# Queries and keys of a four-layer conditioned sequence kernel: from tile to tile instead of through HBM scratch, with a new order of the work

## The chip, the cores and the metric

The kernel runs on 1 core of one Trainium2 chip. The metric is the device time of one execution in microseconds (us), lower is better. Engines are named TensorE (PE), VectorE (DVE), ScalarE (ACT), GpSimd (POOL) and SyncE (SP, which only issues DMAs here).

## The reference

The input x has 16 batches of 256 rows and 256 columns, with a conditioning vector of 64 and one of 256 per batch. Four layers follow each other; nothing passes between batches.

```python
# L0: weights of the batch from a hypernetwork
Wd_b = Wd + 0.1 * (h_lang @ Wdd.T + bdd);  Wu_b = Wu + 0.1 * (h_lang @ Wdu.T + bdu)
x = x + relu(x @ Wd_b.T + bd) @ Wu_b.T + bu
# L1: LayerNorm with weight and bias, plus tanh(cond @ lin_w.T + lin_b), weight and bias again
# L2: 16 heads of 16 columns, all weights shared, gates g1 b1 g2 b2 a1 a2 from the conditioning
h = layernorm(x) * g1 + b1;  q, k, v = split(h @ W_qkv.T + b_qkv)
x = x + (softmax(q @ k.T / 4) @ v @ W_o.T + b_o) * a1
h = layernorm(x) * g2 + b2
x = x + (gelu_tanh(h @ W_f1.T + b_f1) @ W_f2.T + b_f2) * a2          # 1024 wide
# L3: RMSNorm with a scale of the batch, gated GELU, activations rounded to 8 bits, ternary weights
val, gate = split(h @ up_w.T);  y = quant(val * gelu(gate)) @ ternary(down_w).T + x
```

## The kernel before

**Stages and turns.** A batch passes four stages: A (L0, L1 and the queries, keys and values), B (attention), C (output projection and feed-forward of L2) and D (L3). Turn t works on batch t in A, t-1 in B, t-2 in C and t-3 in D, so there are 19 turns: turns 3 to 15 have all four stages, turns 0 to 2 fill the pipeline and turns 16 to 18 drain it. Steps have names such as `A.q` (the queries' product) or `C.f0` (first quarter of the feed-forward's first product). In what order each engine takes the steps is written out by hand in the strings `HEAD` (turns 0 to 5), `FULL` (one turn, repeated from 6 to 12) and `TAIL` (the rest); each engine waits on semaphores and works in its order.

**Precision.** Most products are done on fp32r pairs: a high part (ACT copies it) and a low part (DVE or POOL subtracts), three products for one (`three`, L528). The weights of L2 and L3 are split in this way in turns 0 to 2: `W.qkv`, `W.fa` (first feed-forward weight), `W.up` (128x4096), `W.f2` (POOL, one instruction), and the ternary weight (`W.abs`, `W.tern`).

**Queries and keys.** The scores are one product over 4 x 16 = 64 rows of `Qp` against `Kp`: row 4i is the high part of head row i, 4i+1 and 4i+2 pair high and low parts, and row 4i+3 of `Qp` first holds zero and later the maximum of the score row (`B.m`, which comes back through `mt`), against ones in `Kp`. `B.s` makes the scores for the maximum (eight pairs of heads, in four steps, L658; DVE reduces each pair, L1180), `B.t` makes them again, with the maximum subtracted, for the exponential (L680, ACT L902), `B.o` weights the values (L692). To interleave the rows, SP stores the parts to `qk_scratch` in HBM (`A.qs`, `A.ks`: four DMAs) and loads them back (`A.ql0` to `A.kl3`: eight DMAs of 256 KB, 128 partitions each). PE's `B.s0` waits for the two DMAs of heads 0 (`heads_in[0]`).

**The start.** The batch's L0 weights are generated ahead of turn 0: 16 chunks of 1 MB (`hyper`) are loaded, multiplied (`generate`, L538), copied to `gen`, and the rows of batch 0 and 1 go from `gen` to `cur` and `second` (`first_rows`, L381 and L382, 8 partitions each). `store_rows` (L422) writes `gen` to HBM for the other batches. `A.down` (L596) waits for `cur_ready`; `A.up` is L602, `A.ht` (transposes) L609. `C.proj`, the first step of C, is L703, and marks a turn below.

Of the kernel before, what the change touches and what calls it, by code (L numbers as in the profile page):

```python
# [5 lines left out]
F32 = mybir.dt.float32  # L6
F32R = mybir.dt.float32r
BF16 = mybir.dt.bfloat16
ALU = mybir.AluOpType
# [3 lines left out]
P = 128  # L13
NB = 16
# [50 lines left out]
def at(steps, name, b):  # L65
# [8 lines left out]
        0: W.store0 A.load W.f0 W.up A.qs A.ks A.ql0 A.kl0 A.ql1 A.kl1 A.kl2 A.ql2 A.ql3 A.kl3 1: W.late B.m0 2: C.tc 1: A.load B.m1 A.qs A.ks A.ql0  # L74
        A.kl0 A.kl1 A.kl2 A.ql1 A.kl3 A.ql2 A.ql3 2: B.m0 A.load A.qs B.m1 A.ks A.ql0 A.kl0 3: C.tc 2: A.kl1 A.ql1 A.kl2 A.ql2 A.ql3 A.kl3 3: A.load
        B.m0 A.ks B.m1 A.qs A.kl0 D.y0 A.ql0 4: C.tc 3: A.ql1 A.ql2 D.y1 A.ql3 A.kl1 A.kl2 A.kl3 4: B.m0 A.load A.qs B.m1 A.ks A.ql0 A.kl0 A.kl1
        A.ql1 5: C.tc 4: D.y0 A.kl2 D.y1 A.ql2 A.kl3 A.ql3 5: B.m0 A.load A.qs B.m1 A.ks D.y0 A.ql0 A.kl0 6: C.tc 5: A.ql1 A.ql2""",
    "PE": """
        0: A.down A.up A.ht A.q A.k A.v 1: A.down A.up B.s0 B.s1 A.ht B.m0 B.s2 B.s3 A.q A.k B.m1 B.t0 B.t1 B.o0 B.t2 B.t3 B.o1 A.v 2: C.proj A.down
        A.up B.s0 C.ht B.s1 C.f0 C.f1 C.f2 C.f3 B.m0 A.ht B.s2 W.abs B.s3 A.q A.k B.m1 B.t0 A.v C.g0 B.t1 C.g1 B.o0 C.g2 B.t2 C.g3 B.t3 3: A.down 2:  # L80
        B.o1 C.xt 3: B.s0 A.up C.proj D.u0 B.s1 D.u1 C.ht D.u2 C.f0 C.f1 C.f2 C.f3 B.m0 A.ht B.s2 D.u3 B.s3 D.qt0 A.q A.k B.m1 D.y0 B.t0 A.v C.g0
        B.t1 C.g1 D.qt1 B.o0 C.g2 B.t2 C.g3 B.t3 D.y1 B.o1 C.xt 4: A.down B.s0 C.proj D.u0 A.up D.u1 C.ht B.s1 D.u2 C.f0 C.f1 C.f2 C.f3 B.m0 A.ht
        B.s2 D.u3 B.s3 A.q D.qt0 A.k D.y0 B.m1 A.v B.t0 C.g0 B.t1 C.g1 D.qt1 B.o0 C.g2 B.t2 C.g3 B.t3 D.y1 B.o1 C.xt 5: A.down B.s0 C.proj D.u0 A.up
        D.u1 C.ht B.s1 D.u2 C.f0 C.f1 C.f2 C.f3 B.m0 A.ht B.s2 D.u3 B.s3 D.qt0 A.q A.k""",
    "ACT": """
        0: W.qkv A.down A.lnb A.ht A.q W.fa A.k A.v 1: A.down W.up A.lnb A.ht A.q B.t0 B.t1 B.t2 B.t3 A.k W.f2 B.t4 B.t5 B.t6 B.t7 A.v 2: A.down
        C.lnb C.ht C.f0 C.f1 A.lnb C.gh0 C.f2 A.ht C.f3 A.q C.gh1 A.k B.t0 B.t1 B.t2 B.t3 A.v B.t4 B.t5 B.t6 B.t7 3: A.down 2: C.xt 3: D.u0 C.lnb
        D.u1 C.ht D.u2 C.f0 C.f1 A.lnb C.gh0 C.f2 A.ht D.u3 C.f3 D.qt0 A.q C.gh1 A.k B.t0 B.t1 B.t2 B.t3 D.qt1 A.v B.t4 B.t5 B.t6 B.t7 C.xt 4: D.u0
        A.down C.lnb D.u1 C.ht D.u2 C.f0 C.f1 A.lnb C.gh0 C.f2 A.ht D.u3 C.f3 A.q D.qt0 A.k C.gh1 B.t0 B.t1 A.v B.t2 B.t3 D.qt1 B.t4 B.t5 B.t6 B.t7
        C.xt 5: A.down D.u0 C.lnb D.u1 C.ht D.u2 C.f0 C.f1 A.lnb C.gh0 C.f2 A.ht D.u3 C.f3 D.qt0 A.q C.gh1 A.k B.t0 B.t1 B.t2 B.t3 A.v D.qt1 B.t4  # L90
        B.t5 B.t6 B.t7 C.xt 6: A.down D.u0 C.lnb D.u1 C.ht D.u2 C.f0""",
    "DVE": """
        0: A.up A.lna A.lng A.ln A.cur W.qkv A.q A.k 1: W.fa A.up A.lna A.lng A.ln W.up B.s0 B.s1 B.s2 B.s3 B.p0 B.m0 B.s4 B.s5 B.s6 B.s7 B.p1 B.m1
        A.cur A.q B.o1 A.k B.o3 2: C.proj C.ln A.up B.s0 A.lna A.lng B.s1 B.s2 B.s3 A.ln W.abs B.p0 B.m0 B.s4 B.s5 B.s6 B.s7 B.p1 B.m1 A.q A.k
# [74 lines left out]


def cond_seq_kernel(nc, xT, x, hyper, base, cols, k64, rows, w_qkv, w_o, w_f1, w_f2, w_up, w_down, out,
                    rows_scratch, cur_scratch, qk_scratch):
    ctx = ExitStack()
    with ctx:
        def sb(name, shape, dt):
# [1337 lines left out]
```

## Time and profile before

| | |
|---|---|
| median of 3 runs | 881.86 us (879.83 to 883.41) |
| profiled execution | 881.95 us, span 880.1 us |
| PE busy | 798.5 us, 91% of the span |
| DVE, ACT, POOL busy | 555.9, 554.7, 324.1 us |
| mean granted TensorE clock | 0.943 of full speed |
| DMA | 118.50 MB in 56207 packets |

The span is the time from the first to the last instruction of one profiled execution; its own time is 1.85 us longer. All times in rows are us from the span's start. The granted clock has two levels, 0.5 and 1.00 of full speed (1.2 and 2.4 GHz). SP's DMA issues are not counted as busy time, but its queue (SPq) has rows of its own: start and duration of each issue.

### The profile page before, as it was taken

What the parts mean: (1) busy time and instruction counts of PE and PEld (TensorE: products, weight loads), DVE (VectorE), ACT (ScalarE), POOL (GpSimd) and SP (SyncE); (2) the same over time, 40 slices, a digit from 0 to 9 for tenths busy, and PEclk for the clock granted to TensorE, in tenths of its full rate; (3) what the DMA queues carried; (4) which work ended last, traced back from release to release, by engine and by line L of the source; (5) the groups of instructions that cost most, each with busy time, mean ns of one, the idle gap of its engine ahead of it and who ended that gap; (6) DMA issues with size and microseconds to landing.
All of it is one profiled execution on the core that took longest, in us unless ns stands there. A gap on an engine that the chain in (4) does not pass through costs nothing.

```text
span 880.1 us, 16405 instructions
## 1 busy us (share of the span) xinstructions
PE 798.5 (91%) x6108; PEld 634.1 (72%) x6108; DVE 555.9 (63%) x1063; ACT 554.7 (63%) x844; POOL 324.1 (37%) x398
## 2 busy tenths in 40 slices
PE   6753377999999999999999999999999999999977
PEld 4103256778787878787878788888788887877664
DVE  1313856677767768585858585858586867675424
ACT  1012343668695858685867777676868676867652
POOL 1003423253534344443434352625252535232330
PEclk9855767999999999999999999999999999999998
DMA  9989633434243332425151515141524423220000
GB/s 344 386 325 355 260 127 109 145 106 136 97 136 112 128 121 99 150 86 163 69 179 50 195 49 170 56 171 59 168 77 153 143 96 106 106 94 9 25 13 12
DMA packets 56207, 118.50 MB, mean 135 GB/s; under 512 B 6112, under 2 KB 11616, under 8 KB 53424
## 3 DMA queue, kind: packets, MB, share of 16 engines
q1 hardware_dynamic: 56128, 117.46, 38.6%
q8 instruction: 48, 0.79, 0.4%
q14 instruction: 31, 0.25, 0.1%
HBM read 82.23 MB, written 34.16 MB: 132 GB/s over the span
## 4 chain that ended last, share of the span: by engine, by line
PE 77%; DVE 5%; issue 5%; ACT 4%; POOL 4%; DMA 4%; SPq 1%; POOLq 0%; DVEq 0%; ACTq 0%
PE bank L528 41%; PE pair_s L692 6%; PE pair_t L528 5%; PE bank L789 3%; PE pair_s L680 3%; PE bank L703 3%; DMA hyp<-in_hyper 2%; PE pair_s L658 2%; PE bank L781 2%; PE pair_t L680 2%; PE bank L596 2%; PE bank L602 1%; DVE nmax L1180 1%; PE pair_t L658 1%; DVE hd L1248 1%
## 5 line engine op out<-in xcount | busy, mean ns | idle before, releaser
L1398 POOL TENSOR_TENSOR G_lo<-G,G_hi 128x512 fp32r<-128x512 f32 x64 | 81.9, 1293 | 117.6 <-ACT G_hi L922 117.6
L528 PE MATMUL bank<-wup_hi,hD_hi 128*128 128x512 f32 x256 | 110.5, 432 | 3.8 <-POOL hD_lo L1371 3.1
L528 PE MATMUL bank<-wup_lo,hD_hi 128*128 128x512 f32 x256 | 101.8, 397 | 0.0
L528 PE MATMUL bank<-wup_hi,hD_lo 128*128 128x512 f32 x256 | 101.7, 397 | 0.0
L902 ACT ACTIVATE Pr<-pair_s 128x1024 f32<-128x1024 f32 x64 | 65.7, 1027 | 44.3 <-PE pair_s L680 44.0
L1408 POOL TENSOR_TENSOR x<-x,gated 128x512 f32<-128x512 f32 x16 | 20.4, 1274 | 165.6 <-DVE gated L1238 165.6
L1180 DVE TENSOR_REDUCE nmax<-pair_s 128x4 f32<-128x1024 f32 x64 | 77.9, 1217 | 4.5 <-PE pair_s L658 4.2
L1180 DVE TENSOR_REDUCE nmax<-pair_t 128x4 f32<-128x1024 f32 x64 | 77.7, 1214 | 0.0
L528 PE MATMUL bank<-wf_hi,G_hi 128*128 128x256 f32 x256 | 76.9, 300 | 0.9 <-ACT G L917 0.8
L1204 DVE STREAM_TRANSPOSE oq<-pair_s 128x512 f32<-128x512 f32 x32 | 22.9, 717 | 78.8 <-PE pair_s L692 78.8
L949 ACT ACTIVATE gl<-bank,rsD 128x512 f32<-128x512 f32 x64 | 43.7, 683 | 45.2 <-PE bank L528 44.9
L528 PE MATMUL bank<-wf_lo,G_hi 128*128 128x256 f32 x256 | 71.7, 280 | 0.0
L528 PE MATMUL bank<-wf_hi,G_lo 128*128 128x256 f32 x256 | 71.7, 280 | 0.0
L1248 DVE SCALAR_TENSOR_TENSOR hd<-bank,rsD,gl 128x512 f32<-128x512 f32 x64 | 47.8, 746 | 33.7 <-PE bank L528 25.6
L692 PE MATMUL pair_s<-Pr,Va 128*32 128x256 f32 x1024 | 64.9, 396 | 1.0 <-ACT Pr L902 0.9
L902 ACT ACTIVATE Pr<-pair_t 128x1024 f32<-128x1024 f32 x64 | 65.3, 1021 | 0.0
L528 PEld LDWEIGHTS bank<-wup_hi,hD_hi 128*128 128x128 f32 x256 | 48.5, 189 | 18.2 <-POOL hD_lo L1371 3.4
L528 PEld LDWEIGHTS bank<-wup_lo,hD_hi 128*128 128x128 f32 x256 | 48.5, 190 | 11.8
L528 PEld LDWEIGHTS bank<-wup_hi,hD_lo 128*128 128x128 f32 x256 | 48.8, 191 | 9.7
L528 PEld LDWEIGHTS bank<-wf_hi,G_hi 128*128 128x128 f32 x256 | 48.2, 188 | 8.1 <-issue 2.5
L957 ACT ACTIVATE qT<-bank 128x1024 bf16<-128x1024 bf16 x32 | 32.7, 1023 | 26.0 <-PE bank L781 26.0
L692 PEld LDWEIGHTS pair_s<-Pr,Va 128*32 128x32 f32 x1024 | 29.8, 113 | 26.1 <-ACT Pr L902 7.9
(192 smaller groups left out, 2251.7 us busy)
## 6 DMA issues: line engine op xcount, KB each, us to landing
hyp<-in_hyper SPq DMA_DIRECT2D x16, 1024.0 KB, 10.0
Qp<-qk_scratch SPq DMA_DIRECT2D x64, 256.0 KB, 4.7
Kp<-qk_scratch SPq DMA_DIRECT2D x64, 256.0 KB, 4.6
qk_scratch<-q_hi SPq DMA_DIRECT2D x16, 512.0 KB, 2.8
qk_scratch<-k_hi SPq DMA_DIRECT2D x16, 512.0 KB, 3.2
tC<-rows_scratch SPq DMA_DIRECT2D x16, 384.0 KB, 4.5
xT_t<-in_xT SPq DMA_DIRECT2D x16, 256.0 KB, 4.5
x_t<-in_x SPq DMA_DIRECT2D x16, 256.0 KB, 4.6
```

The costliest lines, as they stand in the source:

```text
L528: mm = pe.matmul(dst, l, r, start=first and i == 0, stop=last and i == 2)
L658: mm = pe.matmul(pair[p % 2][:, half, r * L:(r + 1) * L], Qp[lo:lo + KR, 1 - par, p, r * P:(r + 1) * P], Kp[lo:lo + KR, 1 - par, p, :], st ...
L680: mm = pe.matmul(pair[p % 2][:, half, k * L:(k + 1) * L], Kp[lo:lo + KR, 1 - par, p, k * P:(k + 1) * P], Qp[lo:lo + KR, 1 - par, p, :], st ...
L692: mm = pe.matmul(bank[1][32 * j:32 * j + 32, (g % 2) * L:(g % 2 + 1) * L], Va[:, 1 - par, k, VW * (4 * g + j):VW * (4 * g + j) + 2 * DH], ...
L703: mm = pe.matmul(bank[5][:, r * D:(r + 1) * D], oT[:, k, r * P:(r + 1) * P], wo[:, k, :], start=k == 0, stop=k == KT - 1)
L789: mm = pe.matmul(bank[6][:, 0:D], qT[:, k, :], wq3[:, k, :], start=k == 0, stop=k == FT - 1)
L902: act.activation(Pr[:, p % 4, :, :].rearrange("p a n -> p (a n)"), pair[p % 2][:, :, :].rearrange("p a n -> p (a n)"), ACT.Exp, scale=DH * ...
L949: act.activation(gl[:, n % 2, :], bank[6][:, :], ACT.Gelu, scale=rsD[:, 1, n // 2:n // 2 + 1]).then_inc(act_d, 1)
L957: act.activation(qT[:, :, :].rearrange("p k n -> p (k n)"), bank[7][:, :].bitcast(BF16), ACT.Copy).then_inc(act_d, 1)
L1180: dve.tensor_reduce(nmax[:, n % 2, :, p % GP, :], pair[p % 2][:, :, :].rearrange("p a (r n) -> p a r n", r=RT), AX.X, ALU.max, negate=True ...
L1248: dve.scalar_tensor_tensor(hd[:, (n % 2) * HALF:(n % 2 + 1) * HALF], bank[7][:, :], rsD[:, 1, n // 2:n // 2 + 1], gl[:, n % 2, :], ALU.mul ...
L1398: pool.tensor_tensor(G_lo[:, 2 * i:2 * i + 2, :], G[:, 2 * i:2 * i + 2, :], G_hi[:, 2 * i:2 * i + 2, :].bitcast(F32), ALU.subtract).then_i ...
```

## The change

1. Queries and keys: `qk_scratch` goes. SP copies each part straight from `q_hi`, `q_lo`, `k_hi`, `k_lo` into the interleaved rows of `Qp` and `Kp`, 32 partitions to every fourth partition, 64 KB each: 8 DMAs for `A.qh0`, 4 for `A.ql0`, 8 for `A.kh0`, 4 for `A.kl0`, and 2 small ones that zero the maximum's rows again, so 26 in place of 12. ACT and DVE now guard `q_hi` and the others by PE's last `B.s` of the batch before.
2. Rows: the 16 issues for `second` leave the loop ahead of turn 0 and come in turn 0 (`W.second0`); the load of `wqkv_raw` goes behind the last `first_rows`.
3. Weight splits: `W.up`, the first feed-forward weight, `W.f2` on POOL and the ternary rounding are cut in 2 to 4 pieces each and put at other places; `W.up`'s load comes behind `A.kl0` of turn 0. `W.qkv` on DVE waits for POOL's `nb1`.
4. Unused products: `keep_busy(n)` issues n float32 products of 128x256 on TensorE, whose result nobody reads, in the generation loop and in turn 0.
5. New `HEAD`, `FULL` and `TAIL` for all engines.

```diff
 FULL "SP":
-        -1: A.kl1 D.y1 A.kl2 A.ql3 A.kl3 0: B.m0 A.load A.qs B.m1 A.ks D.y0 A.ql0 A.kl0 1: C.tc 0: A.ql1 A.ql2""",
+        -1: A.qh0 B.m1 A.kh0 A.kl0 D.y0 0: C.tc -1: A.ql0 D.y1 0: B.m0 A.load""",
 FULL "PE" (turned round; one step moved):
-        ... C.g1 B.o0 D.qt1 C.g2 B.t2 ...
+        ... C.g1 D.qt1 B.o0 C.g2 B.t2 ...
 FULL "DVE" (turned round; one step moved):
-        ... D.quant1 D.y0 B.o1 A.cur C.g3 D.y1 B.o3 ...
+        ... D.quant1 B.o1 D.y0 A.cur C.g3 D.y1 B.o3 ...
 HEAD "SP":
-        0: W.store0 A.load W.f0 W.up A.qs A.ks A.ql0 A.kl0 A.ql1 A.kl1 A.kl2 A.ql2 A.ql3 A.kl3 1: W.late B.m0 2: C.tc 1: A.load B.m1 ...
+        0: W.f0 W.zero0 W.store0 W.second0 A.load A.qh0 A.ql0 A.kh0 A.kl0 W.up 1: A.load B.m0 W.late A.qh0 B.m1 A.ql0 2: C.tc 1: A.kh0 A.kl0 2: ...
 HEAD "DVE":
-        ... 1: W.fa A.up A.lna A.lng A.ln W.up B.s0 B.s1 B.s2 B.s3 B.p0 B.m0 B.s4 B.s5 B.s6 B.s7 B.p1 B.m1 A.cur A.q B.o1 A.k B.o3 2: C.proj C.ln A.up B.s0 ...
+        ... 1: A.up A.lna A.lng A.ln B.s0 B.s1 B.s2 B.s3 B.p0 B.m0 B.s4 B.s5 B.s6 B.s7 B.p1
+        B.m1 W.fone1 A.cur W.upper0 A.q W.upper1 B.o1 A.k W.upper2 B.o3 W.upper3 2: C.proj B.s0 C.ln A.up A.lna B.s1 ...
 HEAD "PE":
-        2: C.proj A.down A.up B.s0 C.ht B.s1 C.f0 C.f1 C.f2 C.f3 B.m0 A.ht B.s2 W.abs B.s3 A.q A.k ...
+        2: C.proj B.s0 A.down A.up C.ht B.s1 C.f0 C.f1 C.f2 B.m0 W.abs A.ht B.s2 C.f3 B.s3 A.q A.k ...
 TAIL "PE", turns 15 and 16: A.v of turn 15 now between C.xt and the next C.proj
...
+            def zero_rows():
+                sp.wait_ge(zero, 6)
+                sp.dma_start(none_scratch, x3[0:2, 0].rearrange("p r n -> p (r n)").unsqueeze(1).to_broadcast([2, 4, HALF])).then_inc(planes_out, 16)
+                for u in range(2):
+                    for j in range(4):
+                        sp.dma_start(Qp[3:P:4, u, 2 * j:2 * j + 2, :].bitcast(F32), x3[0:32, 0]).then_inc(planes_out, 16)
...
+            def place(dst, part, rows, par):
+                for j in range(4):
+                    for r in rows:
+                        sp.dma_start(dst[r:P:4, par, 2 * j:2 * j + 2, :].bitcast(F32), part[32 * j:32 * j + 32, :, :].bitcast(F32)).then_inc(heads_in[j], 16)
...
+                    elif (stage, what) == ("A", "qh"):
+                        past(sp, pe_t, PE_T, f"t{NP - 1}", a, 2)
...
+                        for half in range(2):
+                            sp.dma_start(Qp[64 * half + 3:64 * half + 8:4, par, :, :].rearrange("p c n -> p (c n)").bitcast(F32),
+                                         none_scratch.rearrange("q j n -> q (j n)")).then_inc(heads_in[0], 16)
                         sp.wait_ge(act_a, at(ACT_A, "qhi1", a))
+                        place(Qp, q_hi, (0, 1), par)
...
+            def keep_busy(n):
+                for _ in range(n):
+                    pe.matmul(bank[7][:, 0:D], ident, wo[:, 0, :], start=True, stop=True)
             for c in range(6, NCH):
                 generate(c)
+                keep_busy(1 if c < NCH - 1 else 6)
...
                     mm.then_inc(pe_a, 1)          # a_up: keep_busy(15) if a == 0; a_ht: keep_busy(4) if a == 0
...
-                    pe.wait_ge(heads_in[n], 32 * b + 32)
+                    pe.wait_ge(heads_in[n], (128 if n == 0 else 96) * (b + 1))
```

## Rows read from the trace of the kernel before

**Rows 1.** The page: busy time and share, granted clock in 40 slices.
```profile
PE 798.5 (91%) x6108; PEld 634.1 (72%) x6108; DVE 555.9 (63%) x1063; ACT 554.7 (63%) x844; POOL 324.1 (37%) x398
...
PEclk9855767999999999999999999999999999999998
```
**Rows 2.** Windows: length, busy PE PEld DVE ACT POOL, clock, DMA share, GB/s.
```profile
44.00:66.00 22.00, 11.61 (x48) 2.18 (x44) 3.37 (x5) 3.27 (x4) 1.32 (x1) 0.50 0.90 325
...
88.00:110.00 22.00, 8.76 (x49) 5.95 (x48) 18.12 (x25) 8.64 (x11) 8.84 (x8) 0.71 0.70 260
...
132.00:154.00 22.00, 16.69 (x102) 13.81 (x91) 14.82 (x29) 7.42 (x14) 8.26 (x14) 0.78 0.33 109
...
220.00:242.00 22.00, 22.00 (x159) 17.38 (x159) 16.00 (x34) 13.88 (x23) 11.28 (x17) 1.00 0.29 97
```
**Rows 3.** Timeline of PE, C.proj of turns 2, 3, 15, 16, 17.
```profile
135.55 1.89 PE L703 MATMUL bank<-wo,oT 128*128 128x256 f32 x8
...
182.49 1.89 PE L703 MATMUL bank<-wo,oT 128*128 128x256 f32 x8
...
731.81 1.99 PE L703 MATMUL bank<-wo,oT 128*128 128x256 f32 x8
...
778.03 1.99 PE L703 MATMUL bank<-wo,oT 128*128 128x256 f32 x8 [0.39 <-DVE oT L1216]
...
819.67 1.99 PE L703 MATMUL bank<-wo,oT 128*128 128x256 f32 x8 [1.48 <-DVE oT L1216]
```
**Rows 4.** Timeline of SP's queue, 51 to 68 us: start, duration, issue.
```profile
51.16 0.43 SPq L414 DMA_DIRECT2D wqkv_raw<-in_w_qkv  x1
...
60.11 0.56 SPq L381 DMA_DIRECT2D cur<-gen  x1
...
61.80 3.86 SPq L422 DMA_DIRECT2D cur_scratch<-gen  x4
65.71 2.12 SPq L424 DMA_DIRECT2D qk_scratch<-x  x1
```
**Rows 5.** Timeline of PE, turns 0 and 1; in brackets idle time and what ended it.
```profile
64.45 2.05 PE L596 MATMUL bank<-xT_t,cur 128*128 128x256 f32 x4 [5.13 <-DVE cur L1096]
67.06 2.08 PE L602 MATMUL bank<-cur,dn 128*128 128x256 f32 x4 [0.56 <-ACT dn L855]
78.69 1.12 PE L609 MATMUL bank<-small,x 128*128 128x128 f32 x4 [9.56 <-ACT x L865]
...
96.91 0.51 PE L658 MATMUL pair_s<-Kp,Qp 64*128 64x256 f32 x4 [3.87 <-DMA Kp<-qk_scratch]
```
**Rows 6.** Timeline of DVE, turn 1.
```profile
97.85 4.65 DVE L1077 TENSOR_TENSOR wup_lo<-wup_raw,wup_hi 128x4096 fp32r<-128x4096 f32 x1
102.42 1.21 DVE L1180 TENSOR_REDUCE nmax<-pair_s 128x4 f32<-128x1024 f32 x1
```
**Rows 7.** Timeline of POOL, turn 0.
```profile
74.87 1.71 POOL L1341 TENSOR_TENSOR rsA<-mvA,one_neg 128x2 f32<-128x2 f32 x1
```
**Rows 8.** Timeline of PE, first instruction of A.q in turn 2.
```profile
159.61 0.58 PE L528 MATMUL bank<-hA_hi,wqkv_hi 128*128 128x256 f32 x1
```
**Rows 9.** Timeline of SP's queue in one full turn.
```profile
483.76 0.38 SPq L442 DMA_DIRECT2D qk_scratch<-q_hi  x1
...
485.83 1.29 SPq L495 DMA_DIRECT2D Qp<-mt  x2
...
498.11 0.32 SPq L512 DMA_DIRECT2D tC<-rows_scratch  x1
```
**Rows 10.** Timeline of PE: B.s0 and C.proj behind that turn.
```profile
502.27 0.50 PE L658 MATMUL pair_s<-Kp,Qp 64*128 64x256 f32 x4
```
**Rows 11.** SP's issues by tile: duration ns min/median/max, first and last start.
```profile
L382 SPq DMA_DIRECT2D second<-gen x16: 563/575/612, 10.4 to 60.7; - x16
...
L451 SPq DMA_DIRECT2D Qp<-qk_scratch x64: 320/432/1674, 92.1 to 776.5; - x64
```
**Rows 12.** The tile q_lo: its store from issue to landing.
```profile
DMA to landing us min/median/max: 2.2/2.6/4.3
```

## What the change should do to the time

> **What bounds the kernel now.** I read four views. First the page: TensorE is busy 91% of the span, no other engine more than 63%, and its granted clock is at half speed only in the first fifth and in the last slice [rows 1]. Second the windows: between 220 and 242 us TensorE is busy all 22.00 us at clock 1.00, while DMA uses 0.29 of its time; at 44 to 66 and 88 to 110 us it is busy 11.61 and 8.76 of 22 us, at clocks 0.50 and 0.71 [rows 2]. Third TensorE's timeline at C.proj, which marks the turns: from 182.49 to 731.81 us there are 12 turns of 45.78 us; turn 2 takes 46.94 us though it has no stage D; turn 15 takes 46.22, turn 16 41.64, and the rest to the end of the span 60.5 us [rows 3]. So the middle is TensorE's own work, and only three places have room: the start up to 182.49 us, the last 148 us, and nothing else. Fourth the queue of SP, since the change puts most of its new instructions there.
>
> **The middle, 182 to 732 us.** The change takes no product away here and adds none; it moves D.qt1 ahead of B.o0 on TensorE and B.o1 ahead of D.y0 on VectorE. Gain: nothing. What can be lost is time at B.s0, which waits for heads 0. SP now issues 26 DMAs where it issued 12, and the four of A.ql0 stand last, behind C.tc. The store of q_hi, the first thing that SP does once the queries are there, starts at 483.76 us, and B.s0 of the next turn at 502.27 us [rows 9, 10]. Between them SP must do: 8 placements and 2 zeroings, B.m1 (1.29 us for two, so 0.65 each), 12 placements of the keys, D.y0, C.tc, and one placement of q_lo. What is one placement worth? No row shows a copy of 32 partitions to every fourth one. From below, loads of 128 partitions took a median of 0.432 us (0.320 when nothing stood ahead) [rows 11]; from above, the copies that write 8 partitions took 0.575 us [rows 11] and those into two partitions 0.65 us [rows 9]. With the 0.05 us between two issues that is a pitch of 0.48, 0.62 or 0.70 us. The low rows write many partitions, the high ones few; 32 is nearer to the first kind in shape (one run of 2 KB per partition, no cut in two), so I take 0.48, and keep 0.70 for the range.
> With 0.48: 8 x 0.48 + 2 x 0.70 = 5.2 us, B.m1 1.4, keys 12 x 0.48 = 5.8, together 12.4, so 496.2; D.y0 is written to HBM some 0.4 us later. C.tc went at 498.11 because it waits for VectorE's gate [rows 9], and that step keeps its place. The first placement of q_lo starts at 498.5. A store of q_lo took 2.6 us from issue to landing (2.2 at least, 4.3 at most) [rows 12], so heads 0 are there at 501.1, 1.2 us ahead of need. B.m1 goes out some 3 us later than today; its reader is B.t2, and B.t0, A.v, C.g0, B.t1, C.g1, D.qt1, B.o0 and C.g2 stand ahead of that on TensorE. Sum of the middle: 0.
> The Trainium skill, in "DMA: Bandwidth & Descriptors", section "Why a DMA increments its semaphore by 16 and not by 1", says that a DMA of a hardware queue runs on at most 16 engines, as many as divide its slowest dimension, and that the issuing sequencer itself writes the rest of the semaphore's increment when they are fewer. By that rule 32 partitions get all 16 and the price of the 128-partition rows, and 8 or 2 partitions the higher one; the rows agree (0.432 against 0.575 and 0.65 us), but none has 32.
>
> **The start.** Three things stand on the way to turn 1's scores.
> (a) Turn 0 on TensorE. The copy of the last rows is issued at 60.11 us, with wqkv_raw (issued at 51.16) still ahead of it [rows 4], and A.down starts at 64.45 [rows 5]. With that load behind it the copy lands sooner, by about 1 us (4.34 us from its issue to A.down, against 2.2 for the quickest landing [rows 12] and VectorE's combine); but the six unused products now stand there. A.down's two products take 2.05 us at half clock [rows 5], so six take 6.1 us at half clock and 3.1 at full; after a last generation that ends at 59.3 us (64.45 less 5.13 idle) they end between 62.4 and 65.4. I take a gain of 0.8 us, between -1 and +2. If they bring the clock up, A.down and A.up save 1.03 us each, A.ht 0.5 [rows 5]. The 15 behind A.up (15.4 us at half, 7.7 at full clock) lie in an idle gap of 9.56 us [rows 5]: at full clock they cost nothing, at half they push A.ht back by 5.8 us. GpSimd's mean step took 1.71 us [rows 7] while VectorE split wqkv; VectorE now waits for GpSimd, which should give about 1.5 us back.
> (b) SP in turn 0. It now has more ahead of the heads than TensorE. From 60.7 us on: tA, wqkv, f0 3 x 0.48 = 1.4; the zero rows 0.7 + 8 x 0.48 = 4.5; the four stores 3.9 [rows 4]; 16 rows of `second` x 0.62 = 9.9 [rows 11]; tA, xT, x 1.4; A.qh0 5.2, A.ql0 1.9, A.kh0 3.8. That is 32.0 us; the first placement of A.kl0 starts at 92.7 us and lands 2.6 later: 95.3. One issue behind the four stores took 2.12 us instead of 0.43 [rows 4], so the queue can hold SP back; I add 1.2 and take 96.5. B.s0 runs there at 96.91 today [rows 5]. So all of (a) ends in a wait for heads.
> (c) VectorE in turn 1. Today its maximum of the first scores starts at 102.42 us, since the split of wup (4.65 us) stands ahead of it [rows 6], and that of the first feed-forward weight ahead of A.up. Both go behind B.m1, into the time in which TensorE makes A.q and A.k and ScalarE the exponentials. The maxima then start 0.5 us behind B.s0, at 97.0: a gain of 5.4 us, and B.m0, B.m1, B.t0 to A.v and C.proj hang on this chain one after the other. The maxima start between 95.8 (no hold-up) and 99.0 us, a gain of 3.4 to 6.6.
> (d) Turn 2. A.q starts 24.1 us behind C.proj [rows 3, 8], while TensorE is idle 5.3 us of the window 132 to 154 us, which is also partly at half clock [rows 2]. The new order gives VectorE B.s0 right behind C.proj's gate instead of behind A.up, and leaves C.f3 for the wait on the third maximum. I take half of the idle time, 2.5 us; bounds 0 and 5.3. The rounding of the ternary weight moves in pieces into places where TensorE has C.g, whose products need nothing of VectorE; it stays hidden.
> Sum of the start: -7.9 us.
>
> **The end.** TensorE waits 0.39 us for oT at turn 16's C.proj and 1.48 us at turn 17's [rows 3]. A.v of turn 15, 12 products, goes into the first wait. In turn 17 D.u3 goes behind C.f3, so the feed-forward, on which the last batch hangs, no longer stands behind 24 products. I take -2.0 us, between 0 and -4.
>
> **Sum.** The profiled execution took 881.95 us, 0.1 over the median of the runs. 881.95 - 7.9 - 2.0 = 872.0 us.
>
> **Rivals.**
> 1. *SP becomes the bound of every turn.* Each turn's B.s0 waits for q_lo. Speaks for it: 26 issues in 18.5 us. Against it: SP has 1.2 us in hand at a pitch of 0.48, and C.tc's wait hides most of a dearer one. With pitch p, q_lo's first copy starts at 483.76 + 20p + 3.6 (zeroings, B.m1, D.y0 and C.tc) and must not be later than 502.27 - 2.6 = 499.67; that is p = 0.615. At 0.70 it starts at 501.4, 1.7 us late, and 12 turns lose 20 us: 872 + 20 = 892. It turns the sign at p = 0.66 (0.8 us x 12 = 9.9). Chance 12%.
> The Trainium skill, same page, section "Anatomy of one DMA", gives a fixed 2 us and a transfer of 860 KB for half of the bandwidth, which speaks against 24 copies of 64 KB for four stores and eight loads. If they ran one by one, 26 x 2.15 = 56 us would be longer than a turn; the trace disagrees as to the queue: a DMA takes 2.6 us to land [rows 12], and SP issues the next 0.48 us behind it without waiting.
> 2. *The start gives less.* The clock stays at half, the 15 products push A.ht back by 5.8 us, SP is held up by the stores, and turn 1's scores start where they do today. Left are the end and turn 2: 872.0 + 5.4 = 877.4; with turn 2 giving nothing, 879.9. For it: SP's chain is as long as today's. Chance 20%.
> 3. *More than that.* Turns 1 and 2 run at full clock, since there is less waiting: at clocks of 0.71 and 0.78 [rows 2], 12.8 and 9.7 us of the two windows pass at half speed, 5.1 + 7.4 = 12.5 us of it busy at the windows' shares, and half of that would go: 872 - 6 = 866. Chance 15%.
> 4. *Nothing is moved:* the queue is not on the path and the orders are worth nothing: 881. Chance 7%.
>
> My forecast (868 to 877) has 46%. The range to 861 and 884 holds it with rivals 2, 3, 4 and the mild half of 1. What a measurement of this kernel tells from no change is about 0.5%, 4.4 us. Faster by more: forecast, rival 3, and two thirds of rival 2: 0.74. Same: the rest of 2, rival 4 and a little of 1: 0.14. Slower: 0.12.
>
> **What will show it.** Turns in the middle stay at 45.8 us from C.proj to C.proj, with no wait of L658 for a DMA into Qp or Kp except in turn 1; if there is one in each turn, rival 1 holds. Placements issue at a pitch near 0.48 us. In turn 1, B.s0 ends a wait for a DMA at about 96.5 us and the first L1180 starts right behind it; the clock is full between A.up and A.v of turn 0. C.proj of turn 2 comes at about 130 us, that of turn 3 at 174.6, that of turn 15 at 724. The sum is wrong if SP's issues cost another amount than the rows of other shapes, if stores hold SP back by more than 2 us, or if the orders written for other costs make new waits in turns 3 to 5, which no row of before can show.

## The result: 2% slower

Median of the changed kernel 899.66 us (897.52 to 901.15, 4 runs), of the kernel before 881.4 us (4 runs): ratio 1.020, 95% interval 1.017 to 1.023. The prediction said 872.0 and 861 to 884. The profiled execution took 897.52 us, its span 895.7 us against 880.1.

The page first: busy TensorE, its clock, and the chain of work that ended last, by engine. Before, that chain was TensorE for 77% and SP's queue for 1%.

```profile
PE 808.5 (90%) x6176; PEld 643.8 (72%) x6176; DVE 557.6 (62%) x1067; ACT 551.8 (62%) x842; POOL 321.9 (36%) x401
...
PEclk9998587999999999999999999999999999999998
...
PE 49%; SPq 17%; ACT 10%; issue 10%; DMA 7%; DVE 4%; POOL 3%; POOLq 0%; DVEq 0%; ACTq 0%
```

The same windows as in [rows 2].

```profile
44.00:66.00 22.00, 16.29 (x85) 9.55 (x82) 7.73 (x16) 3.15 (x4) 2.65 (x4) 1.00 0.91 325
...
88.00:110.00 22.00, 9.62 (x37) 6.09 (x38) 11.12 (x22) 3.98 (x7) 5.90 (x9) 0.50 0.60 189
...
220.00:242.00 22.00, 19.48 (x114) 15.68 (x107) 15.17 (x32) 10.92 (x21) 11.73 (x18) 0.92 0.23 61
```

The window at 44 has the full clock that the unused products were to give. The one at 88 now passes wholly at the lower level, 0.50 (1.2 GHz), where it was 0.71. And the one at 220, in which TensorE had been busy for all 22.00 us, has 19.48.

TensorE's timeline, with B.s0 (L664) and C.proj (L709), answers to [rows 3, 10].

```profile
132.23 1.99 PE L709 MATMUL bank<-wo,oT 128*128 128x256 f32 x8 [0.45 <-DVE oT L1232]
...
176.88 1.99 PE L709 MATMUL bank<-wo,oT 128*128 128x256 f32 x8 [0.40 <-DVE oT L1232]
...
224.75 0.60 PE L664 MATMUL pair_s<-Kp,Qp 64*128 64x256 f32 x4 [2.52 <-DMA Kp<-k_lo]
...
225.71 3.32 PE L709 MATMUL bank<-wo,oT 128*128 128x256 f32 x8
...
462.63 0.51 PE L664 MATMUL pair_s<-Kp,Qp 64*128 64x256 f32 x4 [1.09 <-DMA Qp<-q_lo]
...
753.35 0.50 PE L520 MATMUL bank<-wup_hi,hD_hi 128*128 128x512 f32 x1 [1.75 <-DVE hd L1264]
...
793.66 1.99 PE L709 MATMUL bank<-wo,oT 128*128 128x256 f32 x8
...
836.06 1.99 PE L709 MATMUL bank<-wo,oT 128*128 128x256 f32 x8 [1.48 <-DVE oT L1232]
```

Three differences make the whole change of the span (turn t is counted from its C.proj to the next one). Up to C.proj of turn 3: 176.88 - 182.49 = -5.6 us. From there to C.proj of turn 16: 616.8 us against 778.03 - 182.49 = 595.5, so +21.2. From there to the end: 102.0 us in both, so 0. Sum +15.6, and the spans differ by 15.6.

The waits of TensorE, summed: us in total, times, longest.

```profile
PE pair_s L664 <- DMA Kp<-k_lo: 12.2, 3, 8.3
PE bank L596 <- DMA xT_t<-in_xT: 9.7, 1, 9.7
PE pair_s L664 <- DMA Qp<-q_lo: 9.4, 10, 1.4
```

B.s0 waits in ten turns for q_lo, the wait that rival 1 named. That is the mechanism; the next rows say why it exists. SP's queue over one middle turn, which answers to [rows 9]:

```profile
438.40 1.18 SPq L467 DMA_DIRECT2D Qp<-none_scratch  x2
442.87 5.44 SPq L449 DMA_DIRECT2D Qp<-q_hi  x8
448.35 1.37 SPq L487 DMA_DIRECT2D Qp<-mt  x2
449.82 4.98 SPq L449 DMA_DIRECT2D Kp<-k_hi  x8
454.89 2.45 SPq L449 DMA_DIRECT2D Kp<-k_lo  x4
457.39 0.58 SPq L508 DMA_DIRECT2D out_y<-x  x1
458.07 0.40 SPq L504 DMA_DIRECT2D tC<-rows_scratch  x1
458.57 2.39 SPq L449 DMA_DIRECT2D Qp<-q_lo  x4
```

And all placements of q_hi and of q_lo: duration of the issue min/median/max in ns, then time from issue to landing, which answer to [rows 11, 12].

```profile
L449 SPq DMA_DIRECT2D Qp<-q_hi x128: 476/594/1432, 86.3 to 791.7; - x128
...
DMA to landing us min/median/max: 2.0/2.1/3.6
```
```profile
L449 SPq DMA_DIRECT2D Qp<-q_lo x64: 470/593/1658, 91.3 to 797.8; - x64
...
DMA to landing us min/median/max: 2.1/2.4/5.0
```

Two things are to be seen. A placement is issued every 0.63 us (12 of the keys from 449.82 to 457.39: 7.57 / 12), and the eight of q_hi ahead of them every 0.68 us, not every 0.48. And the one placement that B.s0 needs last, q_lo's first, is issued at 458.57 and lets B.s0 go at 462.63, 4.06 us later, while q_hi's land in 2.1. It is queued 0.5 us behind tC, a read of 384 KB. The other nine times that B.s0 waits for q_lo, it goes 3.5 to 4.0 us behind the issue, except at 272.49 us, where tC is issued behind the copies of q_lo: 2.1 us. Without its wait of 1.09 us B.s0 would run at 461.54, so the copy has 2.97 us and takes 4.06. Both the pitch and the landing were taken too small; experiments 1, 8 and 11 take them apart.

### The profile page after: what moved, and what is told of

It is laid out like the page before. It is cut to its first block, busy times and chain, and to the rows that moved or that the text cites. A ratio compares the mean times of both kernels' runs of the same rounds, so it can differ in the third digit from the quotient of the medians.

```text
span 895.7 us, 16730 instructions
## 1 busy us (share of the span) xinstructions
PE 808.5 (90%) x6176; PEld 643.8 (72%) x6176; DVE 557.6 (62%) x1067; ACT 551.8 (62%) x842; POOL 321.9 (36%) x401
## 4 chain that ended last, share of the span: by engine, by line
PE 49%; SPq 17%; ACT 10%; issue 10%; DMA 7%; DVE 4%; POOL 3%; POOLq 0%; DVEq 0%; ACTq 0%
PE bank L520 26%; SPq L449 11%; PE pair_t L520 4%; DMA Qp<-q_lo 4%; PE pair_s L698 3%; PE bank L709 3%; ACT G L923 2%; PE pair_s L664 2%; DMA hyp<-in_hyper 2%; SPq L420 2%; ACT G_hi L928 1%; PE pair_s L686 1%; PE bank L602 1%; PE bank L795 1%; DVE nmax L1196 1%
## 5 line engine op out<-in xcount | busy, mean ns | idle before, releaser
L520 PEld LDWEIGHTS bank<-wup_hi,hD_hi 128*128 128x128 f32 x256 | 48.8, 191 | 22.1 <-DVE hd L1264 4.9
L698 PE MATMUL pair_s<-Pr,Va 128*32 128x256 f32 x1024 | 63.1, 387 | 0.6 <-ACT Pr L908 0.5
L520 PEld LDWEIGHTS bank<-wup_lo,hD_hi 128*128 128x128 f32 x256 | 49.0, 191 | 11.9
L664 PE MATMUL pair_s<-Kp,Qp 64*128 64x256 f32 x256 | 34.1, 344 | 24.9 <-DMA Kp<-k_lo 12.2
L520 PEld LDWEIGHTS bank<-wf_hi,G_hi 128*128 128x128 f32 x256 | 48.1, 188 | 10.3 <-issue 5.6
L664 PEld LDWEIGHTS pair_s<-Kp,Qp 64*128 64x128 f32 x256 | 20.8, 196 | 43.1 <-issue 15.0
```

The costliest lines, as they stand in the source:

```text
L520: mm = pe.matmul(dst, l, r, start=first and i == 0, stop=last and i == 2)
L664: mm = pe.matmul(pair[p % 2][:, half, r * L:(r + 1) * L], Qp[lo:lo + KR, 1 - par, p, r * P:(r + 1) * P], Kp[lo:lo + KR, 1 - par, p, :], st ...
L698: mm = pe.matmul(bank[1][32 * j:32 * j + 32, (g % 2) * L:(g % 2 + 1) * L], Va[:, 1 - par, k, VW * (4 * g + j):VW * (4 * g + j) + 2 * DH], ...
```

## The experiments

Times are medians; a ratio is to the kernel before on the same chip, with its 95% interval. "C.proj 3" is the start of C.proj in turn 3.

**1. Half of the placements late (e1_halves).** The 24 copies are kept, but those of heads 4 to 7 go out behind D.y1.

```
-def place(dst, part, rows, par):
-    for j in range(4):
+def place(dst, part, rows, par, n):
+    for j in (2 * n, 2 * n + 1):
...
 FULL SP:
--1: A.qh0 B.m1 A.kh0 A.kl0 D.y0 0: C.tc -1: A.ql0 D.y1 0: B.m0 A.load
+-1: A.qh0 B.m1 A.kh0 A.kl0 D.y0 0: C.tc -1: A.ql0 D.y1 A.qh1 A.ql1 A.kh1 A.kl1 0: B.m0 A.load
```

> The changed kernel, with the placements of each batch cut in two: heads 0 to 3 (12 copies) first, at the places where all 24 stood, heads 4 to 7 (12 copies) behind A.ql0 and D.y1. As many copies, bytes and issues as before the cut. Theory 1 (SP issues a copy only every 0.62 us, and q_lo of heads 0 stands last): B.s0 no longer waits, the turns in the middle go from 46.9 back to 45.8 us, the waits of 2.5 and 1.4 us in turns 3 and 14 go with the falls of the clock behind them, and turn 1 starts 4 to 7 us earlier; total 876 to 882 us. Rival 2 (the new orders of the other engines cost the time) and rival 3 (the copies themselves, not their place in the queue): turns stay at 46.5 us or more, total above 893 us.

Measured: 874.06 us, ratio 0.993 (0.991 to 0.996), below the 876 to 882 that was expected. No wait for a placement in the middle, turns 45.8 us (C.proj at 359.51 and 451.19: 91.68 for two). SP's queue and TensorE around the same place in a turn:

```profile
446.23 0.33 SPq L500 DMA_DIRECT2D tC<-rows_scratch  x1
446.66 1.12 SPq L445 DMA_DIRECT2D Qp<-q_lo  x2
```
```profile
450.52 0.51 PE L660 MATMUL pair_s<-Kp,Qp 64*128 64x256 f32 x4
```

SP now stands still before tC, which waits for VectorE's gate, and q_lo has 450.52 - 446.66 = 3.86 us. From C.proj 3 (176.27) to C.proj 16 (771.85) it takes 595.6 us, all of the 21.2 back, while start and end last as long as in the changed kernel (B.s0 of turn 1 comes 5.4 us earlier, at 95.66, but C.proj of turn 2 stays, at 132.36 for 132.23). The middle's loss is the placements ahead of B.s0 and nothing in the new orders of the other engines. The landing of q_lo behind tC is in this trace 3.6 us, so even with SP waiting in front of tC there are 0.26 us in hand, not the 1.2 of the prediction.

**2. The changed kernel with the scratch mechanism of before (e2_scratch).** Four stores and eight loads, and SP's order of before; the other engines' new orders, split weights and unused products stay.

```
-place(Qp, q_hi, (0, 1), par)
+sp.dma_start(qk_scratch..., q_hi...)
...
+sp.dma_start(Qp..., qk_scratch...)
```

> The changed kernel, with queries and keys through the HBM scratch again (4 stores and 8 loads), SP's order for them as in the kernel before; everything else as changed. Theory 1: turns of 45.8 us, total 870 to 878 us, since the start keeps its gains. Rival 2 (the new orders cost the time): turns above 46.5 us, total above 893 us.

Measured: 876.34 us, 0.996 (0.994 to 0.998); C.proj 3 at 171.26 us, 11.2 earlier than before; middle turns 45.78. What the other engines do anew is thus worth 11.2 us at the start, and the placements, with their order in SP's queue and their zero rows, take 5.6 of it back. The total keeps less, since L694 waits 4.7 us for Qp<-mt in turn 16: the old queue order with the new orders of the end.

**3. Before, with the placements alone (e3_place).**

```
-sp.dma_start(qk_scratch..., q_hi...)
+place(Qp, q_hi, (0, 1), par)
 (orders as before)
```

> The kernel before, with the copies from tile to tile alone: qh and ql where the queries' stores stood, kh and kl where the keys' stores stood, all engines' orders as before. Theory 1: 24 copies at 0.62 us and four small ones take SP to about 501.5 us in a turn in which the queries are there at 483.7; B.s0 is just in time or late by up to 0.5 us, but C.tc and D.y0 stand behind the copies and come 3 us late, so turns take 46 to 47.5 us, total 884 to 900 us. Rival 2: the copies cost nothing, 879 to 883 us.

Measured: 889.71 us, 1.011 (1.008 to 1.013). C.proj 3 at 182.58, as before (182.49), and C.proj 16 at 785.28: 602.7 us of middle, +7.2. The placements cost time under either set of orders, less under this one.

**4. Before, with the unused products alone (e4_busy).**

```
+keep_busy(1 if c < NCH - 1 else 6)
...
+keep_busy(15)
...
+keep_busy(4)
```

> The kernel before, with the unused products alone (one behind each generation, six behind the last, 15 behind A.up and 4 behind A.ht of turn 0). Theory (full clock in turn 0 brings the heads of turn 0 some 4 to 5 us forward, but VectorE's split of wup stands ahead of the first maxima): 874 to 880 us. Rival (clock gain is swallowed by the split of wup): 880 to 882 us. Rival (the products delay A.down and A.ht): above 883 us.

Measured: 877.86 us, 0.997 (0.995 to 0.999). A.q of turn 0 starts where it did, but B.s0 of turn 1 at 95.59 instead of 96.91 [rows 5] and C.proj 3 at 181.54, 1 us earlier. The trace is of the slowest of the ten runs, 880.72 us, so it shows less than the median does. In this kernel the maxima don't follow B.s0 at once: the split of wup still stands in front of them, as (c) of the prediction has it:

```profile
96.80 4.64 DVE L1089 TENSOR_TENSOR wup_lo<-wup_raw,wup_hi 128x4096 fp32r<-128x4096 f32 x1
101.36 1.21 DVE L1192 TENSOR_REDUCE nmax<-pair_s 128x4 f32<-128x1024 f32 x1
```

**5. The start: zero rows on another queue, loads ahead of the stores (e5_start).** From experiment 1.

```
-0: W.f0 W.zero0 W.store0 W.second0 A.load A.qh0
+0: W.f0 W.zero0 W.second0 A.load W.store0 A.qh0
...
+def zero_rows():     # on ScalarE's queue, behind A.down of turn 0
+    act.wait_ge(zero, 6)
+    ... act.dma_start(Qp[3:P:4, u, 2 * j:2 * j + 2, :].bitcast(F32), x3[0:32, 0])
```

> The kernel of e1_halves, with SP's queue of turn 0 relieved: the eight rows of zeros go by ScalarE's queue (behind A.down), and the rows of `second` and the load of batch 1 stand ahead of the four stores of the generated weights. Theory (with TensorE at full clock, turn 0 and 1 are bound by what SP has queued ahead of batch 1 and the heads): xT_t lands near 73 us instead of 87, A.down of turn 1 starts at 79 instead of 89 us and C.proj of turn 2 some 6 to 8 us earlier, total 866 to 869 us. Rival (the stores, 4 MB ahead of the heads in the DMA queues, or another chain, hold the heads back all the same): C.proj of turn 2 moves by less than 2 us, total 872 to 875 us.

Measured: 869.62 us, 0.987 (0.984 to 0.989); C.proj 3 at 171.06, 5.2 us ahead of experiment 1. The gain at C.proj of turn 2 is 5.25 us, under the 6 to 8 expected, and the total just over the expected 866 to 869. So what SP's queue holds ahead of batch 1 and the heads was on the path of the start; the queue's own rows stand below.

**6. Experiment 1 without the unused products (e6_halves_idle).**

```
-keep_busy(1 if c < NCH - 1 else 6)
...
-keep_busy(15)
...
-keep_busy(4)
```

> The kernel of e1_halves without the unused products. Theory (they gain 10 us in turn 0, and SP's queue then eats most of them, as A.down of turn 1 waits 10.15 us for xT_t): 874 to 877 us, a loss of 0 to 3 us. Rival (the unused products are what the gain of the start comes from): 880 us or more.

Measured: 874.55 us, 0.993 (0.991 to 0.994), against 874.06 with them: nothing. TensorE reaches A.q 3.2 us later (76.80 instead of 73.64) and then waits 6.18 us for xT_t instead of 10.15, so A.down of turn 1 starts at 89.42 instead of 88.99.

**7. The rows of `second` back in the generation loop (e7_rows_early).** From experiment 1.

```
 sp.dma_start(cur[8 * c:8 * c + 8, :], gen[0:P:NB, c, :])
+sp.dma_start(second[8 * c:8 * c + 8, :], gen[1:P:NB, c, :])
...
-0: W.f0 W.zero0 W.store0 W.second0 A.load
+0: W.f0 W.zero0 W.store0 A.load
```

> The kernel of e1_halves with the 16 rows of `second` back in the generation loop. In e1_halves they take SP 14.9 us in turn 0, and the last row of `cur` goes out 4 us earlier than before. Theory (SP's queue of turn 0 is the bound): the generation ends 3 to 4 us later, but xT_t and the heads come 8 to 11 us sooner; C.proj of turn 2 at 124 to 128 us instead of 132.4, total 866 to 871 us. Rival (late rows are a gain by themselves): total 876 us or more.

Measured: 869.82 us, 0.987 (0.986 to 0.989); C.proj 3 at 172.08. The generation ends later (A.down of turn 0 at 62.99 instead of 59.30 in experiment 1), and it is 4.2 us to the good all the same: behind the stores the 16 rows cost 14.9 us there. B.s0 of turn 1 now goes at 90.60 without a wait for a DMA, and the next step waits 5.00 us for VectorE's maxima.

**8. What an issue costs (e8_probe).** The kernel before, with three more copies in each middle turn, in time in which SP is idle, into a tile that nobody reads: of four kinds, 82 KB the first and 61 KB the others.

```
+sp.dma_start(probe[:, 160 * i:160 * i + 160], base_c[...])           # L501: tile to tile, 128 partitions
+sp.dma_start(probe[i:P:4, :], base_c[32 * i:32 * i + 32, 0:480])     # L503: 32 to every fourth
+sp.dma_start(probe[32 * i:32 * i + 32, :], base_c[...])              # L505: 32 to 32 adjacent
+sp.dma_start(probe[32 * i:32 * i + 32, :], x[0, 32 * i:...])         # L507: 32 from HBM
```

> The kernel before, with three copies more in each of the turns of batches 3 to 14, issued in SP's idle time ahead of B.m0, of four kinds in turn: 128 partitions x 640 B from tile to tile; 32 partitions x 1920 B to every fourth partition; the same to 32 adjacent partitions; the same from HBM. It asks what makes a placement 0.594 us where a load of 128 partitions is 0.432. If it is the number of partitions, the first kind takes some 0.43 us and the other three 0.59; if the stride, only the second takes 0.59; if the path from tile to tile, all but the last. The time should stay at 881 us.

Measured (one execution, 879.79 us). Duration of the issue, min/median/max in ns:

```profile
L501 SPq DMA_DIRECT2D probe<-base_c x9: 551/596/631, 224.8 to 593.7; - x9
L503 SPq DMA_DIRECT2D probe<-base_c x9: 523/593/597, 270.0 to 639.2; - x9
L505 SPq DMA_DIRECT2D probe<-base_c x9: 580/586/602, 316.7 to 697.6; - x9
L507 SPq DMA_DIRECT2D probe<-in_x x9: 417/435/518, 362.4 to 732.3; - x9
```

Neither the number of partitions nor the stride sets the price: tile to tile takes 0.59 us whether 128 or 32 partitions are written, adjacent or every fourth, and the same 32 from HBM take 0.435. That is the third of the three causes that were expected to be told apart: the path from tile to tile.

**9. Both reliefs of the start (e9_both), and the unused products once more (e10_start_idle).** The first is experiment 5 with experiment 7's rows, the second experiment 5 without the unused products.

```
-0: W.f0 W.zero0 W.second0 A.load W.store0 A.qh0
+0: W.f0 W.zero0 A.load W.store0 A.qh0
+sp.dma_start(second[8 * c:8 * c + 8, :], gen[1:P:NB, c, :])    # in the loop
```

> Half of the placements late, the zero rows on ScalarE's queue, the 16 rows of `second` issued in the generation loop, and xT_t, x_t ahead of the four stores. Theory (SP's queue sets the start as far as turn 1's scores; each part taken out of it helps until VectorE or the generation sets the end): SP is free some 10.7 us sooner than with the zero rows alone moved, but the generation ends 3.5 us later; B.s0 of turn 1 then runs between 85 and 90 us, C.proj of turn 2 at 122 to 126, total 864 to 868. Rival (the two gains are one and the same: whichever part is taken out, the start ends in the chain generation, A.down, heads, VectorE's maxima): C.proj of turn 2 at 127 to 128.5 as with either part alone, total 868.5 to 871.

> As the kernel with half of the placements late and the zero rows on ScalarE's queue, but without the unused products of turn 0. With the old queue order they were worth nothing (874.55 without, 874.06 with), because what they gave was waited away at A.down of turn 1. Theory (their gain was swallowed by SP's queue): with the queue relieved the turn 0 half clock shows, C.proj of turn 2 comes 2 to 5 us later than 127.11, total 872 to 875. Rival (the clock of turn 0 is not on the path at all): C.proj of turn 2 within 1 us of 127.1, total 869 to 871.

Measured: 870.92 us, 0.989 (0.988 to 0.991), C.proj 3 at 172.20; and 869.13 us, 0.987 (0.985 to 0.989), C.proj 3 at 170.85. Both theories fell, and both rivals came true. The two reliefs don't add up: with the rows in the loop SP stands still from 63.0 to 71.5 us, then sends loads and the four stores, and the first heads' copies queue behind those (four of q_hi took 5.04 us). And the unused products are worth nothing here either: without them A.q starts at 76.21 instead of 74.52, and B.s0 of turn 1 at 90.20 instead of 90.47, since in both B.s0 ends a wait for heads 0 (7.18 us with them, 3.66 without).

**10. Where the stores stand (e11_store_late, e12_store_early).** Late is the second kernel of 9 with the stores behind the first half of the heads, early the first kernel of 9 with them in SP's idle time.

```
-... W.second0 A.load W.store0 A.qh0 A.ql0 A.kh0 A.kl0 W.up A.qh1 ...
+... W.second0 A.load A.qh0 A.ql0 A.kh0 A.kl0 W.store0 A.qh1 A.ql1 A.kh1 A.kl1 W.up
```
```
-0: W.f0 W.zero0 A.load W.store0
+0: W.f0 W.zero0 W.store0 A.load
```

> The last kernel (half of the placements late, zero rows on ScalarE's queue, no unused products) with the four stores of 1 MB moved once more, from ahead of the heads of batch 0 to behind them, and the load of wup_raw, which waits for those stores, behind the second half of the heads. Theory (the stores hold SP's queue: 3.8 us for themselves, 2.4 us more than usual for the two zeroings behind them, 1.6 more for the four q_hi copies behind those): B.s0 of turn 1 moves from 90.20 to between 83 and 87 us, where A.up ends; the second half of the heads then stands behind the stores, and wup_raw comes some 15 us later. If nothing of that is late, C.proj of turn 2 comes at 121 to 124 and the total is 864 to 867. Rival (the price is only moved: the second half of the heads or the split of wup_raw in turn 1 waits by as much): C.proj of turn 2 at 126 or later, total 868 or more.

> The kernel with both reliefs (rows of `second` in the generation loop, zero rows on ScalarE's queue, half of the placements late, unused products kept), with the stores ahead of the loads of xT_t and x_t, as the change has them: they then fall into 8.4 us in which SP's queue stands still, from 63.0 to 71.5 us. Theory (what counts is that nothing large stands right ahead of the heads): the four q_hi copies take 2.5 us instead of 5.0, B.s0 of turn 1 comes 2 to 3 us ahead of 91.88, total 867 to 869. Rival (the loads of xT_t and x_t now stand behind the stores, so A.down of turn 1 waits for them and B.s0 gains nothing): A.down of turn 1 later than 85, total 870 to 872.

Measured: late 877.61 us, 0.996 (0.995 to 0.997), C.proj 3 at 178.73; early 867.83 us, 0.987 (0.984 to 0.989), C.proj 3 at 166.52, the lowest median of all, though its interval overlaps those of experiments 5 and 7. TensorE in the late one, heads 2 of turn 1, and in the early one, heads 0 and the next:

```profile
106.90 0.80 PE L647 MATMUL pair_s<-Kp,Qp 64*128 64x256 f32 x4 [8.60 <-DMA Kp<-k_lo]
```
```profile
88.01 0.54 PE L653 MATMUL pair_s<-Kp,Qp 64*128 64x256 f32 x4 [1.53 <-DMA Kp<-k_lo]
...
92.64 0.80 PE L653 MATMUL pair_s<-Kp,Qp 64*128 64x256 f32 x4 [3.66 <-DVE nmax L1191]
```

Late, the rival held: B.s0 of turn 1 gains nothing (90.22 for 90.20), and the price moved to the next heads, which wait 8.60 us (behind the stores four of q_hi took 5.57 us). Early, the theory held in direction: B.s0 3.9 us ahead of 91.88, though A.down of turn 1, at 83.66, does wait 1.49 us for xT_t; the next bound is VectorE, whose normalization of turn 1 stands ahead of the first maxima.

**11. q_lo and the read of tC (e13_ql_first, e14_ql_all).** The changed kernel, 24 copies at their places, with the first one of q_lo ahead of C.tc; and with all four ahead.

```
--1: A.qh0 B.m1 A.kh0 A.kl0 D.y0 0: C.tc -1: A.ql0 D.y1
+-1: A.qh0 B.m1 A.kh0 A.kl0 D.y0 A.ql0 0: C.tc -1: A.ql1 D.y1      # ql0: j = 0, ql1: j = 1, 2, 3
```
```
+-1: A.qh0 B.m1 A.kh0 A.kl0 D.y0 A.ql0 0: C.tc -1: D.y1            # all four
```

> The changed kernel with all 24 placements where they are, but the first of q_lo (the one that B.s0 needs) ahead of C.tc, the read of tC, 384 KB, instead of behind it. In the changed kernel q_lo's first copy was issued at 458.57 us, 0.5 us behind tC, and took 4 to 5 us to land, while q_hi's copies land in 2.1. Theory (what is late is the landing behind tC; SP's queue with its 26 issues would just suffice): that copy is issued 0.6 us earlier and lands in about 2.4 us, B.s0 of turns 6 to 14 waits for nothing, those turns take 45.8 us instead of 46.9, total 886 to 891 (the late turns 3 to 5 stay). Rival (the pitch of 24 copies alone is too much: SP falls behind by about 1 us a turn whatever stands in front): the wait at B.s0 stays near 1 us or goes to the next head, turns 46.5 to 46.9, total 896 to 900.

> The changed kernel with all four copies of q_lo ahead of C.tc, which so goes out 2.4 us later. Theory (landing behind tC): B.s0 free of its wait, turns 45.8 us as with only the first copy moved, if tC's readers (VectorE's first step behind C.proj) have those 2.4 us in hand: total 886 to 891. If they don't, the turns lose what tC is late, up to 2 us each: total 900 to 910. Rival (pitch alone): as above, 896 to 900.

Measured: 887.42 us, 1.008 (1.006 to 1.010), and 895.11 us, 1.018 (1.015 to 1.021). With the first copy alone moved, SP's queue and TensorE, to be laid beside those of the changed kernel above:

```profile
458.78 0.58 SPq L508 DMA_DIRECT2D out_y<-x  x1
459.46 0.47 SPq L449 DMA_DIRECT2D Qp<-q_lo  x1
460.03 0.53 SPq L504 DMA_DIRECT2D tC<-rows_scratch  x1
460.65 1.74 SPq L449 DMA_DIRECT2D Qp<-q_lo  x3
```
```profile
462.40 0.50 PE L664 MATMUL pair_s<-Kp,Qp 64*128 64x256 f32 x4
```

The copy has 462.40 - 459.46 = 2.94 us, as good as the 2.97 of the changed kernel, and B.s0 doesn't wait. D.y0's store stands ahead of it in both kernels, so it's the read of tC that counts. From C.proj 8 at 417.33 to C.proj 14 at 691.97 there are six turns of 45.77 us. So 26 issues at the measured pitch fit into a turn; what made the turns of the middle's regular part late is that the needed copy landed behind a large read. Not all of the loss goes, though: the middle still takes 607.4 us, 11.9 more than before, 8.8 of them in turns 3 to 5 and 2.2 in 14 and 15. Four copies moved cost that gain again: B.s0 is free of q_lo, but tC comes later and turns 6 to 13 still take 45.8 to 48.1 us. TensorE waits more for hd, a tile that VectorE makes in stage D (5.9 us in all ahead of its split products, 3.5 in the changed kernel), and for xc, a tile of stage C that is made with tC (4.9 us, ten times, against 3.0, three times). That tC's delay causes this is the likeliest reading; the chain from tC to hd was not taken apart.

## Why the prediction was wrong

**The middle, forecast 0, measured +21.2 us: the step that failed.** The step says that heads 0 are there 1.2 us ahead of need. It rests on two terms, and both were low.
The pitch of a placement: taken 0.48, measured 0.62 to 0.68, inside its bounds (0.48 to 0.70) but not the value chosen. The choice went by shape, "32 is nearer to the first kind", and shape doesn't matter (experiment 8). The low row was a load from HBM; the higher ones, 0.575 and 0.65 us, were copies from tile to tile, as the placements are. These runs show no effect of the partitions on the issue: from tile to tile it takes 0.575 us at 8 partitions [rows 11] and 0.59 at 32 and at 128. The Trainium skill's rule of how many engines a DMA runs on ("DMA: Bandwidth & Descriptors", section "Why a DMA increments its semaphore by 16 and not by 1") seemed to agree with the choice. The page puts no price of an issue to it, and by these numbers none hangs on it.
The landing of q_lo: taken 2.6 us from a store [rows 12], measured 3.5 to 4.1 from issue to B.s0 behind tC. The prediction named C.tc as the one ahead of q_lo and counted its place in the issue queue, not its 384 KB in the transfer.
Together: q_lo's first copy was to start 14.7 us behind q_hi's (483.76 to 498.5) and started 15.7 behind (442.87 to 458.57), 1.0 more; the landing took 1.5 more; 1.2 us in hand become 1.3 late, and the measured waits are 0.3 to 1.4, five of the ten 1.0 to 1.2.
One term was too high and hid part of this: the two zeroings (1.4 us), which the prediction puts behind the queries, go out ahead of them, at 438.40. Without them rival 1's sum allows a pitch of (12.3 + 1.4) / 20 = 0.685 us instead of 0.615. The 20 placements from 442.87 to 458.57 take 13.05 us, 0.65 each, and in the nine turns in which tC stands ahead of it q_lo's first copy has 2.1 to 3.1 us. The landing of a copy alone, 2.1 us, fits into that, as experiment 11 shows; the 3.5 to 4.1 behind tC don't. In the regular turns rival 1 had the place and the sign, and the term missing in its threshold was the landing.
Of the 21.2 us, 8.7 come from turns 6 to 13, at 46.4 to 47.0 us each, 7.9 from turns 3 to 5 (48.8, 47.4 and 49.1 us) and 4.6 from 14 and 15. At the end of turn 3 it is the issues alone, since k_lo stands last there, with no large read ahead of it:

```profile
207.23 5.17 SPq L449 DMA_DIRECT2D Kp<-k_hi  x8
...
222.47 2.63 SPq L449 DMA_DIRECT2D Kp<-k_lo  x4
```

SP issues without a pause from 207.23 us on, and B.s0 goes 2.28 us behind k_lo's first issue. The 20 placements ahead of that one take 13.1 us. By an estimate from these numbers they would be out 3.5 us sooner at a pitch of 0.48 (20 x 0.48 = 9.6), which is more than the wait of 2.52. New waits in turns 3 to 5 were among the prediction's signs of being wrong.
Behind that wait TensorE's clock is at 0.50 from 225.0 to 228.5 us: the eight instructions of C.proj take 3.32 instead of 1.99 us. The same follows the wait of 1.75 us at 753.35 in turn 15, from 754.0 to 757.5 us. The middle at full clock, as the window at 220 us has it [rows 2], rested on there being no waits.

**The start, forecast -7.9, measured -5.6 us.** Part by part, in the rows of TensorE and of SP's queue in turns 0 and 1 (they answer to [rows 4, 5]):

```profile
58.77 1.10 PE L596 MATMUL bank<-xT_t,cur 128*128 128x256 f32 x4 [1.27 <-DVE cur L1102]
...
61.49 6.64 PE L575 MATMUL bank<-wo,small 128*128 128x256 f32 x30
69.25 0.66 PE L611 MATMUL bank<-small,x 128*128 128x128 f32 x4 [1.12 <-ACT x L872]
...
88.02 2.07 PE L596 MATMUL bank<-xT_t,cur 128*128 128x256 f32 x4 [9.71 <-DMA xT_t<-in_xT]
...
101.02 0.79 PE L664 MATMUL pair_s<-Kp,Qp 64*128 64x256 f32 x4 [8.28 <-DMA Kp<-k_lo]
```
```profile
58.28 6.52 SPq L431 DMA_DIRECT2D Qp<-x  x8
64.84 3.73 SPq L424 DMA_DIRECT2D cur_scratch<-gen  x4
68.61 14.74 SPq L420 DMA_DIRECT2D second<-gen  x16
...
83.88 0.58 SPq L393 DMA_DIRECT2D xT_t<-in_xT  x1
...
86.25 4.97 SPq L449 DMA_DIRECT2D Qp<-q_hi  x8
```

(a) Turn 0 did better than forecast: the clock stays full up to about 81.7 us, where in the kernel before it fell at about 39.4, A.down starts 5.7 us earlier (58.77 for 64.45; the rows of `second` out of the loop are the larger part, 3.7 us by experiment 7), A.ht 9.4 us earlier. Of the 30 instructions of unused products none is in the way.
(b) All of it is waited away, as the step foresaw in kind, but at another place, and the wait is larger: A.down of turn 1 waits 9.71 us for xT_t. SP's chain was costed at 4.5 us for the nine issues of the zero rows and 9.9 for the rows of `second`; they took 7.3 (57.53 to 64.80; 0.82 for each of the last eight) and 14.74. The first is the tile-to-tile pitch again and more; the second is 0.92 a row in the mean behind the 4 MB of stores, though the median issue of this tile is 0.57. B.s0 came at 101.02 instead of 96.5, and the window around it is at half clock.
(c) Its mechanism is right: the maxima start 0.8 us behind B.s0 (101.02), not 5.5 behind it [rows 5, 6].

```profile
101.86 1.23 DVE L1196 TENSOR_REDUCE nmax<-pair_s 128x4 f32<-128x1024 f32 x1 [4.23 <-PE pair_s L664]
```

But B.s0 is 4.1 us later than before, so 0.6 of the 5.4 us were left there (101.86 for 102.42). The gain came in turn 1's later part: C.proj of turn 2 at 132.23 is 3.3 us ahead (forecast some 5.5).
(d) Turn 2: taken 2.5, measured 2.3 (44.65 for 46.94 us). Right.
With the scratch and SP's order for it as before, the same orders give 11.2 us at C.proj 3 (experiment 2), between the forecast and rival 3. Experiments 5, 6, 9 and 10 show what the start hangs on: when the heads of batch 0 land. What TensorE does sooner ahead of that is waited for. Heads 0 alone are not enough: in experiment 1 B.s0 of turn 1 comes 5.4 us sooner, TensorE then waits 2.98 us for VectorE's maxima and 1.18 for heads 2, and C.proj of turn 2 doesn't move. Where the heads come early (experiments 7 and 10's early kernel), VectorE is the next bound, with waits of 5.00 and 3.66 us.

**The end, forecast -2.0, measured 0.** The waits at C.proj of turn 17 stayed (1.48 us, as before), the end behind it is 0.8 us shorter (59.6 for 60.4) and turn 16 takes 0.8 more (42.40 for 41.64). Which move did which wasn't tried, so why the 2.0 us failed to come stays open.

**The rivals.** Rival 1 named the mechanism, at 12%. That its 20 us lie close to the 21.2 measured is luck: it took 1.7 us in each of twelve turns at a pitch of 0.70, and measured are 1.1 us a turn in turns 6 to 13, at a lower pitch and with a dearer landing, and the rest in turns 3 to 5, 14 and 15. Its chance followed the pitch that I had chosen: between 0.48, 0.62 and 0.70 two of the three rows lay at or over its point of 0.615, which was worth more than 12%. Rival 2 fell as to the clock and the 15 products, but SP was held up by the stores, and turn 1's maxima start only 0.6 us sooner, as it had them. Rival 3 fell: turn 1 passes at clock 0.50 and turn 2's first 22 us at 0.77, and even in experiment 2, where the start gains 11.2 us, they are 0.51 and 0.84. The fixed cost of 2 us that the prediction quotes from the Trainium skill ("DMA: Bandwidth & Descriptors", section "Anatomy of one DMA") is given there for GpSimd's path. These copies go by SP's.

## What to carry to other kernels

Cost an issue by what it copies from and to, not by how many partitions it writes, and take the row that agrees with it in that. Where a chain hangs on one small copy, look at what stands ahead of it twice: as time in the issuing queue and as bytes in the transfer; moving one copy ahead of one read gave, by the medians, 12 of the 18 lost us. And before a gain on one engine is booked, follow the queue that feeds its next step: here 9.4 us won at A.ht of turn 0 ended in a wait of 9.7 us in turn 1.

## What the runs showed of the hardware

- SP takes 0.59 us to issue a copy from tile to tile and 0.435 us from HBM, at 32 partitions each (experiment 8); with the gap the pitch of placements is 0.62 to 0.63, and 0.68 for the eight of q_hi at 442.87.
- The issuing queue slows behind large transfers: 0.92 us a row of 16 KB behind 4 MB of stores (0.67 in experiment 5, where the stores came behind them: 10.71 us for 16), and 1.26 us a placement behind the stores and two zeroings (5.04 for four in experiment 9, 2.43 in experiment 10's early kernel).
- A tile-to-tile copy of 64 KB lands in 2.1 us alone (median of q_hi's 128) and in 3.5 to 4.1, from issue to B.s0, behind a read of 384 KB. The Trainium skill, "DMA: Bandwidth & Descriptors", section "Anatomy of one DMA", gives about 2 us of fixed cost for GpSimd's path. No run here has that path; SP's copies come near it with 2.1 us.
- Idle stretches of TensorE of 2.52 us (at 224.75) and 1.75 us (at 753.35) were each followed by some 3.5 us at half clock, while the waits of 0.3 to 1.4 us for q_lo between 272 and 697 us were not.
